# A Fourier tower on one Trainium2 core: the inverse column product in 64x64 tiles, in one piece per pair

## The reference

```python
def _spectral_conv(x, w):
    x_ft = jnp.fft.rfft2(x, norm='ortho')
    out = jnp.einsum('bixy,ioxy->boxy', x_ft[:, :, :20, :20], w.astype(x_ft.dtype))
    out_ft = jnp.zeros((B, 32, 64, 33), x_ft.dtype).at[:, :, :20, :20].set(out)
    return jnp.fft.irfft2(out_ft, s=(64, 64), norm='ortho')

for sw, cw, cb in layers:                       # four of them
    x1 = _spectral_conv(x, sw)
    x2 = jnp.einsum('bchw,oc->bohw', x, cw) + cb[None, :, None, None]
    x = _gelu(x1 + x2)                          # exact gelu
```

## Time and profile before

| | us |
|---|---|
| median of 3 runs | 1637.08 |
| lowest and highest | 1636.37, 1639.5 |
| span of the profiled execution | 1633.9 |
| TensorE matmul busy | 1550.8 (95%) |
| VectorE busy | 1190.1 (73%) |
| ScalarE busy | 603.2 (37%) |

### The profile page before, as it was taken

The page is one execution under the profiler, slowest core; times in us unless marked ns, Lnnn a source line. Parts: engine busy times, 40 slices in busy tenths (PEclk is TensorE's granted clock), DMA queues, the critical chain, the costliest instruction groups (busy, mean ns, idle before and its releaser), DMA issues. The chain is left out here.

```text
span 1633.9 us, 44034 instructions
## 1 busy us (share of the span) xinstructions
PE 1550.8 (95%) x19928; PEld 896.7 (55%) x19928; DVE 1190.1 (73%) x1433; ACT 603.2 (37%) x929; POOL 92.3 (6%) x45
## 2 busy tenths in 40 slices
PE   9899999998999999999999999899999999989996
PEld 3555555555555555565555555777772115963332
DVE  3598899886989989878998998655540115887886
ACT  2433232223332232232322322444449996330221
POOL 1000000000000000000000000000000000007551
PEclk9999999999999999999999999999999999899998
DMA  6333332235655566556556556499998782037430
GB/s 218 114 125 130 128 133 104 120 125 214 247 231 233 207 225 237 215 177 256 214 214 237 222 209 231 139 362 356 354 354 330 255 287 72 1 73 186 110 85 13
DMA packets 59962, 316.30 MB, mean 194 GB/s; under 512 B 16576, under 2 KB 18688, under 8 KB 25984
## 3 DMA queue, kind: packets, MB, share of 16 engines
q1 hardware_dynamic: 36512, 177.99, 32.5%
q10 hardware_dynamic: 23264, 135.49, 20.2%
HBM read 176.09 MB, written 137.36 MB: 192 GB/s over the span
## 5 line engine op out<-in xcount | busy, mean ns | idle before, releaser
L835 ACT ACTIVATE act_c<-slots,conv_b 128x512 f32<-128x512 f32 x512 | 352.6, 689 | 734.0 <-PE slots L550 734.0
L550 PEld LDWEIGHTS slots<-inv_w,inv_out 128*128 128x128 f32 x4096 | 499.4, 196 | 188.2 <-issue 178.9
L550 PE MATMUL slots<-inv_w,inv_out 128*128 128x128 f32 x4096 | 541.8, 287 | 4.8 <-DVE inv_out L725 4.8
L725 DVE STREAM_TRANSPOSE inv_out<-slots 128x1024 f32<-128x1024 f32 x256 | 303.9, 1225 | 98.1 <-PE slots L515 98.1
L701 DVE STREAM_TRANSPOSE turned_h<-slots 128x1024 f32<-128x1024 f32 x200 | 237.9, 1228 | 27.5 <-PE slots L448 26.5
L690 DVE STREAM_TRANSPOSE turned_w<-act_c 128x1024 f32<-128x1024 f32 x192 | 224.9, 1208 | 1.1 <-ACT act_c L835 1.1
L448 PE MATMUL slots<-turned_w,fwd_w 32*64 32x512 f32 x3200 | 200.0, 607 | 3.0 <-DVE turned_h L701 2.5
L707 DVE STREAM_TRANSPOSE modes<-slots 128x640 f32<-128x640 f32 x96 | 81.0, 846 | 79.8 <-PE slots L460 79.8
L460 PE MATMUL slots<-turned_h,fwd_h 64*64 64x320 f32 x1600 | 136.4, 453 | 1.3 <-DVE turned_h L701 1.3
L537 PE MATMUL slots<-act_c,conv_w 32*32 32x512 f32 x3072 | 111.8, 604 | 19.3 <-DVE modes L707 15.4
L515 PE MATMUL slots<-turned_k,inv_h 32*64 32x320 f32 x2048 | 102.3, 455 | 8.3 <-DVE turned_k L715 6.9
(11 more groups left out here) (166 smaller groups left out, 1124.3 us busy)
## 6 DMA issues: line engine op xcount, KB each, us to landing
act_scratch<-act_c ACTq DMA_DIRECT2D x128, 1024.0 KB, 4.8
act_c<-act_scratch SPq DMA_DIRECT2D x128, 1024.0 KB, 5.2
mode_w<-in_sw_dram SPq DMA_DIRECT2D x20, 640.0 KB, 4.4
at_turned<-level_scratch SPq DMA_DIRECT2D x24, 256.0 KB, 4.2
at_ret_t<-level_scratch SPq DMA_DIRECT2D x20, 256.0 KB, 4.4
xin<-in_x_dram SPq DMA_DIRECT2D x4, 1024.0 KB, 8.1
turned_w<-in_x_turned_dram SPq DMA_DIRECT2D x3, 1024.0 KB, 5.9
at_straight<-level_scratch SPq DMA_DIRECT2D x10, 256.0 KB, 4.2
```

Source lines behind the costliest of these rows:

```text
L550: mm = nc.tensor.matmul(banks[:, p, at:at + 128], inv_out[:, t % 2, i, p, :, :, r].rearrange("p b o -> p (b o)"), inv_w[:, i, :], start=Fa ...
L725: nc.vector.transpose(dst, src).then_inc(inv_turned, 1)
L835: nc.scalar.activation(act_c[:, t % RING, :, p, :], banks[:, p, :].rearrange("p (i m) -> p i m", i=2), ACT.Gelu, bias=conv_b[:, l:l + 1]). ...
```

## The change

`inverse_h` no longer makes even and odd sums. Its weights have 64 rows (all row frequencies of one half of the column frequencies) and give the complete sum for one half `s` of the image rows. The table `inv_w` then needs no signs and has 64 rows (stored twice, for the two halves of the partitions) and 64 columns. `inverse_w` is cut into matmuls of 64x64 weights over 64 moving columns: 64 of them per pair in place of 16 with 128x128 weights over 128 columns. Four that follow each other use the four 64x64 parts of the array. Both halves of `inverse_w` (banks 0 and 1, banks 2 and 3) now stand right behind `conv`, and `dft_w` follows them. ScalarE's gelu is issued on two banks at a time, twice per pair in place of four times, and the semaphores `summed` and `act_set` count halves. `keep_busy` multiplies another constant table of the same size.

```diff
             def inverse_h(l, t):
                 for i in range(2):
-                    for kwh in range(2):
-                        for khh in range(2):
-                            b, half = 2 * kwh + khh, khh ^ i
-                            mm = nc.tensor.matmul(banks[half * 64:(half + 1) * 64, 4 + 2 * i + kwh, 0:320],
-                                                  inv_h[b * 32:(b + 1) * 32, l % 2, :],
-                                                  turned_k[b * 32:(b + 1) * 32, t % 2, i * 320:(i + 1) * 320],
+                    for s in range(2):
+                        for kwh in range(2):
+                            rows = slice(kwh * 64, (kwh + 1) * 64)
+                            mm = nc.tensor.matmul(banks[s * 64:(s + 1) * 64, 4 + 2 * i + kwh, 0:320],
+                                                  inv_h[rows, l % 2, s * 64:(s + 1) * 64],
+                                                  turned_k[rows, t % 2, i * 320:(i + 1) * 320],
                                                   start=True, stop=True)
...
-            def inverse_w(l, t, p):
+            def inverse_w(l, t, two):
                 for i in range(2):
                     for r in range(2):
-                        at = i * 256 + r * 128
-                        mm = nc.tensor.matmul(
-                            banks[:, p, at:at + 128],
-                            inv_out[:, t % 2, i, p, :, :, r].rearrange("p b o -> p (b o)"),
-                            inv_w[:, i, :], start=False, stop=True, skip_group_check=True)
+                        for s in range(2):
+                            for half in range(2):
+                                for odd in range(2):
+                                    rows, at = slice(odd * 64, (odd + 1) * 64), i * 256 + r * 128 + s * 64
+                                    mm = nc.tensor.matmul(
+                                        banks[half * 64:(half + 1) * 64, 2 * two + odd, at:at + 64],
+                                        inv_out[rows, t % 2, i, two, s, 2 * half:2 * half + 2, :, r].rearrange(
+                                            "p b o -> p (b o)"),
+                                        inv_w[rows, :], start=False, stop=True, skip_group_check=True)
                 mm.then_inc(summed, 1)
...
                     conv(l, j)
-                    for p in range(2):
-                        inverse_w(l, j, p)
+                    inverse_w(l, j, 0)
+                    inverse_w(l, j, 1)
                     if j >= 2 and not last:
...
                         dft_w(forward(l + 1, j - 2))
-                    for p in range(2, 4):
-                        inverse_w(l, j, p)
                     if j >= 3 and not last:
-                        pe.wait_ge(act_set, after_out(l, j, 1))
+                        pe.wait_ge(act_set, after_out(l, j, 0))
                         dft_h(forward(l + 1, j - 3), (l + 1) % 2)
...
-                    for p in range(4):
-                        act.wait_ge(summed, after_out(l, t, p))
-                        nc.scalar.activation(act_c[:, t % RING, :, p, :],
-                                             banks[:, p, :].rearrange("p (i m) -> p i m", i=2), ACT.Gelu,
+                    for two in range(2):
+                        at = slice(2 * two, 2 * two + 2)
+                        act.wait_ge(summed, after_out(l, t, two))
+                        nc.scalar.activation(act_c[:, t % RING, :, at, :].rearrange("p i q m -> p q i m"),
+                                             banks[:, at, :].rearrange("p q (i m) -> p q i m", i=2), ACT.Gelu,
                                              bias=conv_b[:, l:l + 1]).then_inc(act_set, 1)
```

More of the change, by code:

```diff
@@ L63, in dft_constants @@
     fwd_h = np.zeros((2, 2, 2, 32, 2, 2, 32))
-    inv_h = np.zeros((2, 2, 2, 32, 2, 32))
+    inv_h = np.zeros((2, 2, 2, 32, 2, 2, 32))
     for parity in range(2):
@@ L76, in dft_constants @@
                     fwd_h[parity, :, 1, n, ph, kh % 2, at + 1] = cos[h, kh]
[L77 to L86, removed]
+        for p in range(4):
+            for n in range(32):
+                half, s, q, r = n // 16, n // 8 % 2, n // 2 % 4, n % 2
+                if p // 2 != half:
+                    continue
+                a, b = (p, q) if parity == 0 else (q, p)
+                h = 32 * s + 8 * a + 2 * b + r
+                for kh in range(MODES):
+                    at = kh // 2 * 2
+                    inv_h[parity, :, kh % 2, at, p % 2, 0, n] = cos[h, kh]
+                    inv_h[parity, :, kh % 2, at, p % 2, 1, n] = sin[h, kh]
+                    inv_h[parity, :, kh % 2, at + 1, p % 2, 0, n] = -sin[h, kh]
+                    inv_h[parity, :, kh % 2, at + 1, p % 2, 1, n] = cos[h, kh]
     kw = np.arange(MODES)
@@ L90, in dft_constants @@
     places = 16 * (kwh ^ place % 2) + place
[L91 to L97, removed]
+    inv_w = np.zeros((2, 2, 32, WW))
+    inv_w[:, 0, places] = norm * cos.T
+    inv_w[:, 1, places] = -norm * sin.T
     f32 = np.float32
@@ L225, in tower @@
         fwd_h = sb("fwd_h", [128, 2, 2, 64])
-        inv_h = sb("inv_h", [128, 2, 64])
-        inv_w = sb("inv_w", [128, 2, 128])
+        inv_h = sb("inv_h", [128, 2, 128])
+        inv_w = sb("inv_w", [128, WW])
         lift_w = sb("lift_w", [128, LIFT_E, CH])
@@ L335, in after_inv_turned, with after_out @@
             return l * (2 * PAIRS) + 2 * t + i + 1
-        def after_out(l, t, p):
-            return (l * PAIRS + t) * 4 + p + 1
+        def after_out(l, t, two):
+            return (l * PAIRS + t) * 2 + two + 1
         def after_load(l, t):
@@ L542, in keep_busy @@
                 for _ in range(n):
-                    nc.tensor.matmul(banks[:, b, 384:512], inv_w[:, 0, :], inv_w[:, 0, :], start=True, stop=True)
-            def inverse_w(l, t, p):
+                    nc.tensor.matmul(banks[:, b, 384:512], inv_h[:, 0, :], inv_h[:, 0, :], start=True, stop=True)
+            def inverse_w(l, t, two):
                 for i in range(2):
                     for r in range(2):
-                        at = i * 256 + r * 128
-                        mm = nc.tensor.matmul(
-                            banks[:, p, at:at + 128],
-                            inv_out[:, t % 2, i, p, :, :, r].rearrange("p b o -> p (b o)"),
-                            inv_w[:, i, :], start=False, stop=True, skip_group_check=True)
+                        for s in range(2):
[7 more added lines that the diff above has]
+                                        inv_w[rows, :], start=False, stop=True, skip_group_check=True)
                 mm.then_inc(summed, 1)
@@ L592, in _ @@
                 inverse_h(l, 1)
-                for p in range(1, 4):
-                    inverse_w(l, 0, p)
+                inverse_w(l, 0, 1)
                 for j in range(1, PAIRS):
@@ L623, in _ @@
                     dft_w(ends[1])
-                    pe.wait_ge(act_set, after_out(l, PAIRS - 1, 3))
+                    pe.wait_ge(act_set, after_out(l, PAIRS - 1, 1))
                     keep_busy(4, 3)
@@ L634, in _ @@
                     keep_busy(2, 4)
-            pe.wait_ge(act_set, after_out(LAYERS - 1, PAIRS - 1, 3))
+            pe.wait_ge(act_set, after_out(LAYERS - 1, PAIRS - 1, 1))
             pe.wait_ge(w2_set, 1)
@@ L663, in _ @@
             for _ in range(4):
-                nc.tensor.matmul(banks[:, 0, 0:128], inv_w[:, 0, :], inv_w[:, 0, :], start=True, stop=True)
+                nc.tensor.matmul(banks[:, 0, 0:128], inv_h[:, 0, :], inv_h[:, 0, :], start=True, stop=True)
         def mix_part(u, side, images=slice(0, IMAGES)):
@@ L681, in turn_act @@
             def turn_act(f, t):
-                dve.wait_ge(act_set, after_out(f - 1, t, 3))
+                dve.wait_ge(act_set, after_out(f - 1, t, 1))
                 if t >= 2:
```

18 lines of the change are left out of this document (9 added, 9 removed).

## The result

The changed kernel takes 1756.98 us (median of 4 runs, 1749.51 to 1763.0) against 1636.72 us before (the three runs of the table and one more): a ratio of 1.072, 95% interval 1.068 to 1.076. It is slower by 120 us. The forecast was 1607 us, the range 1590 to 1650, so both the direction and the range were wrong. Two of the kernels further down, `early_dft_h` and `early_col`, had three slow executions between them (one at a lower clock); their medians and ratios are of the other runs.

What follows compares the result with a forecast made beforehand. TensorE was taken to bound the kernel, with VectorE 0.95 us behind, and DMA to bind layer 3 next. Savings of 23.5 + 5.7 + 1.0 = 30.2 us from 1633.9 gave 1603.7, plus 3.2: 1607 us, range 1590 to 1650.

Steps and rivals of the forecast that it cites:

- The first step, what bounds the kernel: TensorE, 95% busy, bounds the kernel with VectorE 0.95 us behind; in layer 3 transfers take 95% of the DMA engines.
- Part 1: Whole `inverse_w` as 64x64 matmuls takes 2.08 us, as long as one half did before.
- Part 2: `inverse_h` on four 64x64 parts grows by 0.56 us, from 0.80 to 1.36 us.
- Part 3: Layers 0 to 2: `inverse_h` waiting for `turn_w` makes the period 9.20 us for 9.48, saving 23.5 us; slack 2.27 us.
- a floor per record: `inverse_w` ahead of `dft_w`: TensorE limits record rate; 18 ns gives 1625 us (0.09), from 20 ns slower (0.18).
- Part 4: Layer 3: DMA engines hold the iteration at 5.75 us, from 5.94, saving 5.7 us over 30 iterations.
- The third rival: Layer 3 not held by the DMA engines; at 5.0 us an iteration 22 us more saved, 1584 us; chance 0.06.
- What would show it: Signs: `inverse_w` about 2.1 us, `inverse_h` 1.36, `turn_inverse` each 9.2; layer 3 at 5.7 to 5.8 with DMA at 98%.
- The rule of 25 ns: Skill page's claim that matmuls never start closer than about 25 ns; `inverse_w` would take 3.2 us, the kernel slower.
- The 3.2 us: Added to the forecast span of 1603.7 us, as the median of timed runs lies that far above the profiled span.

Runs made afterwards that it cites:

- early_dft_h: The kernel before with `dft_h` moved ahead of the second half of `inverse_w`, instruction count unchanged; 1640.7 us, ratio 1.003.
- early_col: The kernel before with `dft_h` ahead of the second half of `inverse_w` and each `inverse_w` matmul split in two by weight columns; 1605.28 us, ratio 0.982.
- after_wide: The changed kernel with `inverse_w` as 64 rows by all 128 weight columns, 32 matmuls a pair in place of 64; 1804.2 us, ratio 1.102.
- col_split: The kernel before, in its old order, with each `inverse_w` matmul split in two by weight columns (128 rows by 64); 1598.37 us, ratio 0.979.

## Why the prediction was wrong

**The first step, what bounds the kernel,** held. **Part 1,** the length of `inverse_w`, was 2.08 us and measured 2.14; with the 0.19 us for the change-over set apart, as there, that is 15 ns a record. **Part 2,** `inverse_h`, was 1.36 and measured 1.31. **Part 3** named the next wait (`inverse_h` behind `turn_w`) and a period of 9.20 us: undisturbed iterations take 9.06. Its slack, 2.27 us for `inverse_w` before `dft_w` delays `turn_w`, is confirmed by `after_wide`. By these steps layers 0 to 2 would each have been 28 x (9.48 - 9.06) = 12 us shorter.

**The step that failed** is one that was not worked out. Part 1 took the instructions as always at hand, so the time to bring them stood in the sum as nothing, without a reason, and only what the array needs was bounded. The runs showed 151.7 us of pauses in its place, where the kernel before has 7.9. The rival "a floor per record" came near: more records than TensorE can take, in `inverse_w` ahead of `dft_w`. But its mechanism was another one. It priced each record alike, and at the 17 ns a record that `inverse_w` showed such a floor costs nothing. The real limit is per block of 256 instructions, and it depends on what else the DMA engines do. The row to see it in was on the page of the kernel before and not read (packets, MB, share of 16 engines):

```profile
q8 instruction: 158, 2.59, 0.6%
```

That is 16 KB a packet and one packet for 256 records. From it, 448 instructions an iteration are 1.75 fetches in 9.1 us, and 320 in a row (`conv` and `inverse_w`) more than one within 3.2 us. In the changed kernel the packet that a pause waits for starts 2.7 us (median) after TensorE entered the block before, in one case of ten over 5.5 us, and TensorE goes on 2.3 us after the packet's start: 5 us for 256 instructions, where the fastest block in the trace went by in 2.2. With small transfers the two are 1.1 and 2.5 us, 3.6 in all. That is why pauses get fewer and shorter there and do not vanish.

**Part 4,** layer 3, counted on the DMA engines as the next bound and on 5.75 us an iteration. It did not come to that, as TensorE stood still instead: 7.7 us an iteration on average. The third rival, a layer 3 of some 5.0 us, did not come true. In `col_split` most iterations of layer 3 take 5.64 us with the full transfers, so the 5.75 was too high as a bound. But 5.64 us is TensorE's own time there: `inverse_w` starts at 1104.00 us, `inverse_h` at 1107.65, `conv` at 1108.55 and `inverse_w` again at 1109.64, one behind the other, and from 1010 to 1180 us `conv` waits for a transfer only twice, 1.9 us in all. What the DMA engines allow below that stays open. Single iterations reach 4.56 us, near the 4.62 of TensorE alone, with the full transfers and with the small ones.

**What would show it** asked for the right views. In undisturbed iterations the lengths for layers 0 to 2 came out near what it names, but in layers 1 and 2 few were undisturbed: the median period is 9.08, 10.26 and 9.84 us in layers 0, 1 and 2. Those for layer 3 (5.7 to 5.8 us, DMA at 98%) did not come out, and the page's "issue" idle time in front of L552 was what did not fit.

**The clock** is a second cost, set off by the first. In the rows of layer 3 it is 0.85 in place of 1.00. Taking the pauses away (small transfers, or half the instructions in layer 3) also takes most of that away, so I hold it for a consequence. How many of the 120 us it makes was not measured alone; as an estimate, 106 us at 1.2 GHz can have cost at most half of that, 53 us.

**The rule of 25 ns** that spoke against the change does not hold for different parts of the array: `inverse_w` ran 128 records in 2.14 us, 17 ns each, and cut `conv` 128 in 1.84. The Trainium skill, page "TensorE: Matmul & The Clock Gate", section "Wait — 56ns, not 53.3ns?", would have forecast a slower kernel and been right by another mechanism than its own.

**The 3.2 us** that the forecast adds to the span compare two different executions; the profiled run of the changed kernel took 1749.51 us with a span of 1747.7, 1.8 us more.

**Still open:** how many blocks ahead the chip asks for, and why a fetch starts so late behind a 1 MB transfer. Both were read from times only. The small transfers have as many packets as the full ones (60056 in both kernels) and only make them shorter, so the amount of data and the size of its packets were not told apart.

## What to carry to other kernels

Splitting a matmul into more and smaller ones costs instructions, and TensorE's instructions come over the same DMA engines as the data. Count them per iteration and in the densest run: here 448 per 9 us with up to 320 in one run lost 120 us, 320 per 9 us with no 256 in less than 3.6 us brought no more pauses than before, and the split that adds fewest instructions (columns of the weights only) gave about 2%. Pauses that end for "issue" in the middle of a block of equal matmuls, at the same record number modulo 256, are the sign.

## What the runs showed of the hardware that was not expected

- The pauses come at one residue modulo 256 of TensorE's records, whatever line stands there: `inverse_w`, `dft_w` or `conv`. Beside 1 MB transfers the longest is 5.4 us in the changed kernel and 6.7 with cut `conv`; with small transfers 1.6 and 2.3.
- No block of 256 is entered sooner than 2.15 us after the start of its packet, in the changed kernel with full and with small transfers.
- Consecutive matmuls on the same 32x32 part do not let the next part start: cut `conv` took 8.05 us with the pieces of a part in a row and 1.84 us with the parts in turn.
- 128 records of 64x64 weights with 64 moving columns take 2.14 us on four parts, 128 of 32x32 with 128 columns 1.84 us on sixteen: 14 to 17 ns a record.
